# Column tiles of 32, one added probability tile and a new step order in a fused AdaLN, path attention and expert kernel

## What is computed

```python
w_down = down_project * (cond @ down_gamma) + cond @ down_beta      # 256 -> 64, per sequence
w_up   = up_project   * (cond @ up_gamma)   + cond @ up_beta        # 64 -> 256
h      = relu(x @ w_down) @ w_up + x
paths  = sigmoid(h @ Wp + bp)                  # 8 heads x 5 levels
agree  = pq * pk + (1 - pq) * (1 - pk)         # every query against every key
sim    = cumprod(agree, -1).sum(-1) / 5        # causal mask
x1     = x + (softmax(sim) @ (h @ Wv)) @ Wo
U      = (cond @ W_dec + b_dec)                # (257, 30), per sequence
z      = x1 @ U[:-1] + U[-1];   y = z @ V      # 256 features
e      = argmax(y @ gate_w.T)                  # one of 8 experts
out    = x1 + y + y @ expert_w[e].T
```

## Time and profile before

| | |
|---|---|
| median of 3 runs | 170.01 us (169.91 to 173.27) |
| profiled execution | 169.74 us |
| its span, first to last instruction | 167.3 us |
| busy: TensorE, weight loads, VectorE, ScalarE, GpSimd | 149.8, 102.3, 75.3, 58.9, 29.1 us |
| mean granted clock of TensorE | 0.99 |

### The profile page before, as it was taken

The page is one execution under the profiler, slowest core; times in us unless marked ns, Lnnn a source line. Parts: engine busy times, 40 slices in busy tenths (PEclk is TensorE's granted clock), DMA queues, the critical chain, the costliest instruction groups (busy, mean ns, idle before and its releaser), DMA issues.

```text
span 167.3 us, 3934 instructions
## 1 busy us (share of the span) xinstructions
PE 149.8 (90%) x1728; PEld 102.3 (61%) x1728; DVE 75.3 (45%) x148; ACT 58.9 (35%) x70; POOL 29.1 (17%) x56
## 2 busy tenths in 40 slices
PE   6989489999965899987999899968999999999893
PEld 6656255654733577555676577646776766667672
DVE  0570708086705854177026365086143754164341
ACT  3004353725730424554430334466223447301010
POOL 8000022003022100250220200250222025200000
PEclk9999999999999999997899999999999999999999
DMA  5999999000220000000000010000011000010111
GB/s 127 295 427 449 387 365 289 16 4 0 33 31 4 0 4 0 4 0 0 4 33 31 31 35 0 4 0 4 11 52 35 31 4 0 4 63 31 63 34 64
DMA packets 7376, 12.42 MB, mean 74 GB/s; under 512 B 1552, under 2 KB 5808, under 8 KB 7232
## 3 DMA queue, kind: packets, MB, share of 16 engines
q10 hardware_dynamic: 2496, 7.23, 11.1%
q1 hardware_dynamic: 4768, 4.89, 9.2%
q0 software_dynamic: 96, 0.05, 0.8%
HBM read 9.95 MB, written 2.22 MB: 73 GB/s over the span
## 4 chain that ended last, share of the span: by engine, by line
PE 76%; DVE 12%; DMA 4%; ACT 3%; issue 2%; SPq 1%; POOL 0%; POOLq 0%; DVEq 0%; ACTq 0%
PE work L539 35%; PE c_ps L539 21%; PE s_ps L539 15%; DVE feat L530 4%; DMA u_scratch<-u_row 2%; PE work L700 2%; DVE h_t L439 2%; DMA u_raw<-u_scratch 2%; PE work L640 1%; DVE rden L404 1%; ACT prob L349 1%; DVE u_w L473 1%; ACT phi_t L374 1%; DVE x_t L519 1%; SPq L285 1%
## 5 line engine op out<-in xcount | busy, mean ns | idle before, releaser
L349 ACT ACTIVATE prob<-s_ps 128x1536 f32<-128x1536 f32 (+1 forms) x24 | 38.2, 1591 | 36.1 <-PE s_ps L539 35.9
L404 DVE RECIPROCAL rden<-c_ps 128x256 f32<-128x256 f32 x16 | 28.1, 1757 | 20.0 <-PE c_ps L539 20.0
L328 POOL TENSOR_SCALAR_AFFINE_SELECT prob<-prob 128x1024 f32<-128x1024 f32 x16 | 18.1, 1132 | 107.1 <-ACT prob L349 107.1
L539 PE MATMUL c_ps<-prob,v_sb 128*32 128x256 f32 (+1 forms) x384 | 26.8, 351 | 0.0
L539 PE MATMUL s_ps<-phi_t 32*128 32x256 f32 (+1 forms) x384 | 24.9, 374 | 1.5 <-ACT phi_t L374 1.0
L539 PE MATMUL c_ps<-prob,ones 128*32 128x256 f32 (+1 forms) x384 | 26.1, 344 | 0.0
L539 PEld LDWEIGHTS s_ps<-phi_t 32*128 32x128 f32 x384 | 17.9, 190 | 9.3 <-issue 5.4
L519 DVE TENSOR_TENSOR x_t<-work,x_t 128x256 f32<-128x256 f32 x16 | 6.8, 423 | 29.3 <-PE work L539 29.3
L539 PE MATMUL work<-ctx_t,mix_sb 128*128 128x256 f32 x64 | 17.8, 401 | 1.2 <-DVE h_t L439 0.8
L539 PEld LDWEIGHTS c_ps<-prob,v_sb 128*32 128x32 f32 x384 | 10.3, 110 | 11.0 <-issue 4.3
L539 PE MATMUL work<-zo_t,gexp 128*128 128x256 f32 x64 | 16.5, 381 | 0.0
(11 more groups left out here) (92 smaller groups left out, 120.1 us busy)
## 6 DMA issues: line engine op xcount, KB each, us to landing
wdec<-in_W_dec ACTq DMA_DIRECT2D x1, 3855.0 KB, 14.8
x_t<-in_x_tr SPq DMA_DIRECT2D x4, 512.0 KB, 9.2
ex_t<-in_expert_tr ACTq DMA_DIRECT2D x1, 2048.0 KB, 23.0
out_x<-x_t SPq DMA_DIRECT2D x16, 128.0 KB, 1.7
mix_sb<-in_mix ACTq DMA_DIRECT2D x1, 776.0 KB, 16.5
lift_sb<-in_lift ACTq DMA_DIRECT2D x1, 384.0 KB, 4.3
w_vl<-in_vl SPq DMA_DIRECT2D x1, 296.0 KB, 5.5
first_sb<-in_first SPq DMA_DIRECT2D x1, 144.0 KB, 4.0
```

The costliest lines, as they stand in the source:

```text
L328: nc.gpsimd.affine_select(out=tri, in_=tri, compare_op=ALU.is_ge, fill=0.0, base=0, pattern=[[0, HG], [0, 2], [1, P]], channel_multiplier= ...
L349: nc.scalar.activation(prob[:, p % 2, :, 0:width(p)], s_ps[:, :, 0:width(p)], ACT.Exp).then_inc(exped, 1)
L404: link(nc.vector.reciprocal(rden[:], c_ps[m % 2][:, CW:2 * CW]))
L539: return nc.tensor.matmul(o, w, r, start=start, stop=stop, skip_group_check=True)
```

## The change

Three things are changed. First, `down`, `VL`, `WoU` and `out` are issued as products of 32 output partitions each, four (the new `tiled`) in place of one; `down` had two of 64. Secondly, for the long chunks a new step `add` has VectorE add the two unmasked probability tiles of the opening pair into `tiles` (128 x 4 x 256); the products with ones are left out in the opening pair's context, and in that of the closing pair one quad with ones on `tiles` stands first. That context waits for the add, and the exp two pairs after the opening one too, since it overwrites what the add reads. Thirdly, the order is new: `phi` follows the scores of pair 5 where it followed the context of pair 3; `zT`, `zs`, `zo` and `zoT` stand elsewhere; `Q`, `Uadd`, `WoU`, `G(0)` and `ubT` too; the outputs of a sequence are spread otherwise.

```diff
+def opening(p):
+    return pair(p)[1][1] == 1 and pair(p)[1][4]
+def adds(p):
+    return sum(opening(i) for i in range(p + 1))
...
     if n1 < B:
         gaps[0] += [("up", n1, 0), ("up", n1, 1)]
+        gaps[4] += [("phi", n1, 0), ("phi", n1, 1)]
     if b == 0:
         gaps[1] += [("VL", n1, 2), ("VL", n1, 3)]
         gaps[2] += [("U", 1)]
         gaps[3] += [("U", 3)]
-        gaps[4] += [("Q",), ("Uadd",)]
-        gaps[5] += [("G", 1)]
+        gaps[5] += [("G", 1), ("Uadd",)]
     elif n1 < B:
-        gaps[1] += [("VL", n1, 0), ("VL", n1, 1)]
+        gaps[1] += [("zs", prv, ALL_T), ("zo", prv, 0), ("zo", prv, 1), ("VL", n1, 0), ("VL", n1, 1)]
         gaps[2] += [("VL", n1, 2), ("VL", n1, 3)]
-    if b == 1:
-        gaps[0] += [("WoU",)]
-    if prv >= 1:
-        gaps[0] += [("out", prv - 1, 3)]
+    else:
+        gaps[1] += [("zs", prv, ALL_T), ("zo", prv, 0), ("zo", prv, 1)]
+        gaps[4] += [("zs", b, FIRST), ("zo", b, 0)]
     if prv >= 0:
-        gaps[4] += [("zoT", prv, 1)]
-        gaps[5] += [("out", prv, 1)]
+        gaps[3] += [("zoT", prv, 0), ("zoT", prv, 1)]
...
-        gaps[4] += [("ubT",), ("G", 0)]
-    if prv >= 0:
-        gaps[1] += [("zT", prv, ALL_T)]
-        gaps[2] += [("zs", prv, ALL_T), ("zo", prv, 0), ("zo", prv, 1)]
-        gaps[3] += [("zoT", prv, 0)]
-        gaps[4] += [("out", prv, 0)]
+        gaps[3] += [("Q",)]
+        gaps[4] += [("G", 0), ("ubT",)]
+        gaps[5] += [("down", n2), ("WoU",)]
+    else:
+        gaps[0] += [("zT", prv, ALL_T)]
+        gaps[3] += [("out", prv, 0)]
+        gaps[4] += [("out", prv, 1)]
         gaps[5] += [("out", prv, 2)]
...
-    if n1 < B:
-        gaps[3] += [("phi", n1, 0), ("phi", n1, 1)]
-    if n2 < B:
+    if prv >= 1:
+        gaps[1] += [("out", prv - 1, 3)]
+    if b >= 1 and n2 < B:
         gaps[5] += [("down", n2)]
     if b == B - 1:
         gaps[2] += [("zT", b, FIRST)]
-        gaps[4] += [("zs", b, FIRST), ("zo", b, 0)]
-        gaps[5] += [("zoT", b, 0), ("out", prv, 3)]
+        gaps[5] = [("zoT", b, 0), ("out", prv, 2), ("out", prv, 3)]
...
+        if _p + 1 < ALL and opening(_p + 1):
+            ORDER += [("add", _p + 1)]
-ORDER += [("out", B - 1, 0), ("zT", B - 1, SECOND), ("zs", B - 1, SECOND), ("zo", B - 1, 1),
+ORDER += [("zT", B - 1, SECOND), ("out", B - 1, 0), ("zs", B - 1, SECOND), ("zo", B - 1, 1),
...
                     if p >= 2:
                         act.wait_ge(summed, p - 1)
+                        if opening(p - 2):
+                            act.wait_ge(added, adds(p - 2))
...
+                elif kind == "add":
+                    p = s[1]
+                    both = prob[:, p % 2].rearrange("p h (s q) -> p h s q", s=2)
+                    dve.wait_ge(exped, p + 1)
+                    nc.vector.tensor_tensor(tiles[:, chunk(p) % 2], both[:, :, 0, :], both[:, :, 1, :], ALU.add
+                                            ).then_inc(added, 1)
...
+            def tiled(o, w, r, start, stop):
+                for j in range(P // DH):
+                    part = slice(DH * j, DH * (j + 1))
+                    ins = mm(o[part], w[:, part], r, start=start, stop=stop)
+                return ins
...
+                if half and last:
+                    pe.wait_ge(added, adds(p))
+                    for h in range(HG):
+                        mm(c_ps[m % 2][DH * h:DH * (h + 1), CW:2 * CW], ones[:], tiles[:, m % 2, h, :],
+                           start=False, stop=False)
...
+                    if half and first:
+                        continue
...
                     for c in range(DC):
-                        for j in range(2):
-                            ins = mm(o[HD * j:HD * (j + 1), 0:T // 2], w_dn[:, b, c, :],
-                                     x_t[:, b, c, T // 2 * j:T // 2 * (j + 1)], start=(c == 0), stop=(c == DC - 1))
+                        for j in range(4):
+                            ins = mm(o[DH * j:DH * (j + 1), 0:T // 2], w_dn[:, b, c, DH * (j % 2):DH * (j % 2 + 1)],
+                                     x_t[:, b, c, T // 2 * (j // 2):T // 2 * (j // 2 + 1)],
+                                     start=(c == 0), stop=(c == DC - 1))
...
-                        ins = mm(o[:, 0:D + H * DEPTH], h_t[:, c, P * t:P * (t + 1)], w_vl[:, c, :],
-                                 start=(c == 0), stop=(c == DC - 1))
+                        ins = tiled(o[:, 0:D + H * DEPTH], h_t[:, c, P * t:P * (t + 1)], w_vl[:, c, :],
+                                    start=(c == 0), stop=(c == DC - 1))
...
-                        ins = mm(o[:, 0:CW], w, r, start=(c == 0), stop=(c == 2 * DC - 1))
+                        ins = tiled(o[:, 0:CW], w, r, start=(c == 0), stop=(c == 2 * DC - 1))
```

More of the change, by code:

```diff
@@ L133 @@
         ORDER += _c
-ORDER += [("out", B - 1, 0), ("zT", B - 1, SECOND), ("zs", B - 1, SECOND), ("zo", B - 1, 1),
+        if _p + 1 < ALL and opening(_p + 1):
+            ORDER += [("add", _p + 1)]
+ORDER += [("zT", B - 1, SECOND), ("out", B - 1, 0), ("zs", B - 1, SECOND), ("zo", B - 1, 1),
           ("out", B - 1, 1), ("zoT", B - 1, 1), ("out", B - 1, 2), ("out", B - 1, 3)]
-NO_BANK = ("scores", "context", "bias", "tanh", "feat", "Uadd", "zo")
+NO_BANK = ("scores", "context", "add", "bias", "tanh", "feat", "Uadd", "zo")
 EARLY = 6
@@ L196, in build @@
         q_bd = sb("q_bd", [P, TT, E])
+        tiles = sb("tiles", [P, 2, HG, CW])
         gexp = sb("gexp", [P, 2, D])
@@ L246, in build @@
         summed = sem("summed")
+        added = sem("added")
         ctx_ready = sem("ctx_ready")
@@ L664, in _ @@
                         for d in range(DC):
-                            ins = mm(o[:, P * c:P * (c + 1)], wo_t[:, d, P * c:P * (c + 1)],
-                                     u_w[:, d].rearrange("p b k -> p (b k)"), start=(d == 0), stop=(d == DC - 1))
+                            ins = tiled(o[:, P * c:P * (c + 1)], wo_t[:, d, P * c:P * (c + 1)],
+                                        u_w[:, d].rearrange("p b k -> p (b k)"), start=(d == 0), stop=(d == DC - 1))
                 elif kind == "G":
```

## The result

The changed kernel takes 155.73 us (median of 4 runs, 155.55 to 156.17). The kernel before, run beside it, had a median of 171.64 us, and the ratio is 0.9166 with a 95% interval of 0.9129 to 0.9203: 8.3% faster. (The ratio compares undisturbed runs alone, and the median of before holds two disturbed ones.) The profiled execution took 155.55 us, its span is 153.4 us. Forecast were 155.0 us and a span of 152.3.

The account below looks back on a forecast made before the run. TensorE, busy 149.8 of 167.3 us, was taken as the bound: less 8.0 of work, less 10.8 of waits and clock, plus 4.0 of new waits gave 152.5 us of span (152.3 taken), 155.0 median; 8 in 10 between 152 and 160.

Parts of the forecast that it names:

- The walk: The new order followed engine by engine with the rows' durations; counting drains singly, it gave 151.6 us of span.
- The products with ones: In each of 8 long chunks TensorE loses two quads of 256 columns and gains one: 3.5 us saved.
- The waits that go: TensorE's waits for ub_col, feat, up's bank, zo and in the tail vanish: 9.3 us, with the clock 10.8.
- the clock: The slow stretch of 7.6 us at 0.78 around a long feat wait goes with that wait: 1.5 us saved.
- The waits that come: New waits of TensorE in the new order, five items from U(3) to the tail: 4.0 us together.
- phi's bank ahead of out(.,1): out(.,1) waits for the bank of phi(.,0), which ScalarE empties after an exp: 0.3 us, twice.
- The one at U(3): add(2) ahead of the copies of U on VectorE makes U(3) wait 1.5 us, 2.0 by the shared-port rule.
- The tiling: Column tiles of 32 save TensorE 2.6 us on out, 1.1 on VL, 0.8 on down and WoU: 4.5 us.
- A: Rival: the tiling does nothing and only the 3.5 us of the ones is saved: 159.5 us, chance 0.12.
- B: Rival: VectorE, with the adds, becomes late for phi or the context behind feat in three batches: 159 us, chance 0.13.
- C: Rival: four tiles fed by the same operand are served in turn: 203 us at twice the time, chance 0.04.
- the waits (2) to (5): Bank waits at phi(1,1) 0.9 us, VL(n,1) 0.3 twice, out(.,1) 0.3 twice; VectorE in the tail 0.4.

Follow-up runs that it names:

- e7: The changed kernel without the first of the eight adds (chunk 2, while U is built): 153.08 us, 0.906 of the kernel before.
- e3: The changed kernel without any add, products with ones for every probability tile as before: 156.58 us, 0.928 of the kernel before.
- e1: The kernel before with only down, VL, WoU and out as column tiles of 32, old order: 166.01 us, 0.981 of the kernel before.
- e11: e8 with phi(n,1) put back behind the scores of pair 5, phi(n,0) left ahead of them: 151.29 us, 0.896 of the kernel before.
- e8: e7 with Q right behind U(3), VL(n,1) behind the context and phi ahead of the scores of pair 5: 151.99 us, 0.900 of the kernel before.
- e9: The changed kernel with only the 16 out steps at full width again: 157.72 us, 0.933 of the kernel before.
- e2: The changed kernel with the tiling alone undone, down in two tiles of 64 again: 159.17 us, 0.943 of the kernel before.
- e4: The new order alone, without tiling and without add: 159.81 us, 0.947 of the kernel before.

## Why the prediction was right

**The walk, by its checkpoint.** The prediction records one, 31 us from scores(9) to scores(15), where the kernel before took 37. Measured were 31.2 (64.91 to 96.07). An "out" takes 1.73 us from start to start among its like (82.03 to 83.76) and 1.84 ahead of scores, both as forecast.

**The products with ones.** 8 x 0.433 us was right by the quad: e7 against e3 gives 3.0 us for seven of them.

**The waits that go.** All went, 9.3 us. For the clock I had taken 1.5 us and tied it to the `feat` wait; e1 shows a like drop behind another wait while the `feat` waits ran at full clock. No drop while TensorE works is in any of the eleven profiles of kernels with the new order; that it hung on this wait is wrong, and which wait brings it is open. The size was right for the profiled execution: from the last transposes of phi to scores(12) it took 76.95 to 84.23 = 7.28 us, and the same steps one sequence later, at full clock, 113.95 to 119.72 = 5.77, 1.5 less. Over the runs it is less: in the three comparisons of e1 to e11 the seven runs of before at a clock of 1.00 took 168.5 us on average (167.9 to 168.8), the eight at 0.99 took 169.4 (168.3 to 170.5).

**The waits that come.** Q, 0.9 forecast, 1.0 measured; VL 0.6 in two, 0.5; phi's bank ahead of out(.,1), 0.6 in two, measured from 76.35 + 0.89 to 77.55, about 0.3 each (0.89 is what that context takes in e8, where the "out" behind it need not wait). Of the 0.4 in the tail 0.2 can be read, ahead of the last zoT. The one at U(3) is the term that was too small: 1.5 us (2.0 by the rule of the shared port), 2.2 measured. The add alone explains it: 2.12 us where I had 1.2 is 0.9 us. `feat` ended 0.4 later than in my walk and TensorE was ready 0.6 later (39.4 and not 38.8), which took 0.2 back. The rule in the Trainium skill, SBUF — State Buffer, the shared port pair, is borne out by this trace in its effect (2.12 us beside a mask, 1.21 without), and the sum by it was the better one; by exclusion for the full length the add that starts 0.59 us into a mask of 1.63 should be late by 1.04, and it was by 0.91. No run was made for this question alone, but the mask behind the second add takes 2.12 us here and 1.10 in e3, which has no adds. The walk missed one more thing here: it had the exp that overwrites what the add reads as later in any case, and at pair 4 ScalarE sat idle for it until 41.10. It ended at 42.98, and TensorE's scores(5), which need it, come at 44.87, so they didn't wait for it.

**The tiling.** I had 4.5 us and it is 3.3, the other term that was off. e9 puts 2.3 us on the "out" steps (forecast 2.6); the other 1.0 is left for VL, down and WoU where I had 1.9, of which 0.3 fall in the opening and are not in this measure. Two errors are visible. "down" was priced at two quads, 0.87 us, against 1.01, but the getting out stays: 83.76 to 84.74 is 0.98, and the saving is 0.03 and not 0.15. In the tail I had booked 0.6 us for six "out" steps; they stand between transposes of their own width there, and had less to win. The 62 ns for a MATMUL without hardware decoding (the Trainium skill, TensorE: Matmul & The Clock Gate, "What happens when you issue a matmul") bind nothing here: the quads of "out" stream at full rate, 16 records in 0.86 us, 54 ns each.

**The rivals.** A falls by e1 and e2, with 3.3 us. B came to pass at U(3) alone; behind `feat` VectorE had time, as in the walk. C falls by the quads of "out": fed by one operand they take 0.43 us as those of a context do.

**The sum.** It was 152.5 us of span, and 153.4 were measured. The tiling was 1.2 us too favourable and U(3) 0.7. The order was 1.6 us better than I had it: from scores(0) on e4 is 146.2 - 136.3 = 9.9 us shorter than the kernel before, and I had 10.8 less 2.5 for the waits (2) to (5), 8.3. The waits that the two profiles list differ by 7.7 us, as forecast (9.3 less the waits for Q and VL); with 1.5 for the clock 0.7 us remain, for which I have no row. The new order also brings steps of one width together, which would have this sign, but this was not tried. The loads were 0.2 us later than in the profile of before. The 0.4 us that are left lie in the adds: 3.5 - 2.2 would leave 1.3 and e2 against e4 shows 0.9. Most of it comes with the first add, which e7 leaves out and gains 2.0 us, where the wait of 2.2 less a quad would be 1.8; its cause stays open. So the near hit is partly luck: 1.9 us too favourable and 1.6 too unfavourable cancel.

## What to carry to other kernels

Read a step's price from start to start in two places, between its like and between strangers: the difference is what the change of the tile width costs, and giving the neighbours one width saved that here and no more. A product moved to another engine pays in full (here 0.43 us each, seven times) where that engine has slack, and turns into a wait where it stands ahead of a copy that a bank hangs on (here 2.2 us, five quads); so place, or leave out, each single one by who waits behind it. When an order is changed, follow the bank and not only the data: all three small waits that came with it, and the one that my own repair brought, were for a bank that the step two before had not given back.

## What the runs showed of the hardware that I had not expected

The price of changing the tile width has a part that does not depend on the widths: 0.11 us on the last quad in front of a 64-wide and of a 128-wide step alike. The part on the other side grows a little with the width: 0.92 us for the half of "out" at 64 columns, 0.96 at 128, 0.86 with no change.

Seven adds took 1.21 to 1.23 us and twelve of sixteen masks 1.10. Where a mask and a VectorE instruction met, the one that came second was late. The first add came 0.59 us behind the start of a mask and took 2.12. The second started 0.06 us ahead of a mask: it took its 1.23, and the mask 2.12. The third started 0.26 us ahead of one, which took 1.92. Without the adds (e3) these two masks take 1.10; that of the first add takes 1.63 either way, and starts beside `feat`. In the tail a step of the `zs` chain with 16 columns, 0.18 us in the last chain, started 0.02 us behind a mask and took as long as the mask:

```profile
47.33 1.23 DVE L509 TENSOR_TENSOR tiles<-prob 128x1024 f32<-128x1024 f32 x1
...
47.39 2.12 POOL L342 TENSOR_SCALAR_AFFINE_SELECT prob<-prob 128x1024 f32<-128x1024 f32 x1 [7.48 <-ACT prob L365]
...
133.79 1.10 POOL L342 TENSOR_SCALAR_AFFINE_SELECT prob<-prob 128x1024 f32<-128x1024 f32 x1 [7.31 <-ACT prob L365]
133.81 1.10 DVE L524 TENSOR_TENSOR key<-hit,rank 128x16 f32<-128x16 f32 x1
...
144.79 0.18 DVE L524 TENSOR_TENSOR key<-hit,rank 128x16 f32<-128x16 f32 x1
```

The granted clock dropped to its lower level for some 3.4 us in the profiles of the two kernels in the old order, each time behind a different wait, and in none of the eleven with the new order, though the changed kernel has a wait of 2.2 us too. Of the runs whose mean clock is listed, 15 of 22 of the kernel before and 3 of 4 of e1 were at 0.99 or below, and 2 of 44 in the new order (both of the changed kernel, 0.989). So the drop is rarer in the new order and not ruled out by it.
